# Preparing the first batch by halves: when tokens are turned, when query and key halves start, and when the value weights are split

## The reference

```python
mod = (silu(c) @ wmod).reshape(2, 6, 1, 256)
sa, ca, ga, sb, cb, gb = ...                       # shifts, scales and gates of a batch
h = layernorm(x) * (1 + ca) + sa
q, k, v = h @ query_proj, h @ key_proj, h @ value_proj   # 16 heads, 16 wide (q, k), 64 wide (v)
x = x + ga * (softmax(q @ k.T / 4, axis=queries) @ v) @ output_proj
h = layernorm(x) * (1 + cb) + sb
x = x + gb * fp4_ffn(h)                            # gate, up and down, quantised to FP4 in blocks of 16
```

## Time and profile before

| what | value |
|---|---|
| median of 3 runs | 1666.05 us (1665.92 to 1666.1) |
| the profiled execution's own time | 1665.84 us |
| its span in the trace | 1664.5 us |
| PE, DVE, ACT, POOL busy over the span | 98%, 94%, 83%, 46% |
| first scores of batch 0 start at | 70.6 us |

### The profile page before, as it was taken

The page is one execution under the profiler, slowest core; times in us unless marked ns, Lnnn a source line. Parts: engine busy times, 40 slices in busy tenths (PEclk is TensorE's granted clock), DMA queues, the critical chain, the costliest instruction groups (busy, mean ns, idle before and its releaser), DMA issues.

```text
span 1664.5 us, 38879 instructions
## 1 busy us (share of the span) xinstructions
PE 1634.2 (98%) x15435; PEld 796.8 (48%) x15435; DVE 1566.7 (94%) x1719; ACT 1377.4 (83%) x2557; POOL 773.6 (46%) x1624
## 2 busy tenths in 40 slices
PE   8999999999999999999999999999999999999999
PEld 7742223322322332673222332222233279999998
DVE  7899999999999999769999999999999969998887
ACT  6599999999999999659999999999999943343334
POOL 3034444444444445303545454566644456654552
DMA  7102111112111112511111112111111454444420
GB/s 243 58 11 73 51 48 46 45 52 67 51 51 53 46 46 77 153 55 40 48 50 45 46 45 71 51 51 52 48 46 45 133 159 127 153 127 133 148 91 23
DMA packets 83109, 123.15 MB, mean 74 GB/s; under 512 B 4712, under 2 KB 69104, under 8 KB 82928
## 3 DMA queue, kind: packets, MB, share of 16 engines
q1 hardware_dynamic: 82512, 120.15, 22.8%
q10 hardware_dynamic: 416, 0.53, 0.1%
HBM read 74.52 MB, written 46.15 MB: 72 GB/s over the span
## 4 chain that ended last, share of the span: by engine, by line
PE 90%; ACT 4%; DVE 2%; POOL 2%; issue 2%; DMA 0%; ACTq 0%; POOLq 0%
PE acc L641 53%; PE slot L612 14%; PE acc L473 12%; PE slot L473 9%; ACT e_sb L929 1%; PE slot L761 1%; ACT ost L951 1%; ACT ost L953 1%; DMA v_sb<-in_wmod 0%; PE slot L494 0%; PE acc L674 0%; POOL e_sb L1611 0%; DVE e_sb L1179 0%; PE acc L713 0%; ACT e_sb L858 0%
## 5 line engine op out<-in xcount | busy, mean ns | idle before, releaser
L1228 DVE TENSOR_REDUCE nm<-slot 128x1 f32<-128x1024 f32 x1024 | 1162.2, 1210 | 18.0 <-PE slot L612 18.0
L929 ACT ACTIVATE e_sb<-slot,nm 128x1024 f32<-128x1024 f32 x1024 | 1132.7, 1124 | 12.5 <-DVE nm L1228 12.5
L641 PE MATMUL acc<-e_sb,vp 64*64 64x512 f32 x8192 | 1065.1, 595 | 20.8 <-ACT ost L953 19.2
L612 PEld LDWEIGHTS slot<-stq,stk 64*64 64x64 f16 x4096 | 115.8, 103 | 674.2 <-ACT e_sb L929 639.6
L612 PE MATMUL slot<-stq,stk 64*64 64x512 f16 x4096 | 404.8, 387 | 0.0
L641 PEld LDWEIGHTS acc<-e_sb,vp 64*64 64x64 f32 x8192 | 281.4, 132 | 147.3 <-issue 58.0
L1545 POOL TENSOR_TENSOR dlt<-nm 128x4 f32<-128x4 f32 x128 | 25.6, 200 | 548.0 <-DVE nm L1228 548.0
L929 ACT ACTIVATION_READ_ACCUMULATOR e_sb<-slot,nm 128x1 f32 x1024 | 215.2, 210 | 0.0
L1536 POOL TENSOR_TENSOR vp<-v_sb,fac 128x512 f32<-128x512 f32 x128 | 133.4, 1042 | 10.2 <-POOL fac L1526 0.3
L1522 POOL TENSOR_TENSOR rtot<-tot,mone 128x4 f32<-128x4 f32 x128 | 132.7, 1036 | 10.0
L1084 POOL TENSOR_TENSOR ost<-ost,ost_hi 128x256 fp32r<-128x256 f32 x128 | 93.4, 730 | 10.3
(11 more groups left out here) (225 smaller groups left out, 1941.5 us busy)
## 6 DMA issues: line engine op xcount, KB each, us to landing
o_r<-o_heads SPq DMA_DIRECT2D x32, 1024.0 KB, 7.2
stk<-qk_parts SPq DMA_DIRECT2D x128, 128.0 KB
o_heads<-ost_hi SPq DMA_DIRECT2D x64, 256.0 KB, 3.4
o_heads<-ost SPq DMA_DIRECT2D x64, 256.0 KB, 4.0
v_sb<-in_x SPq DMA_DIRECT2D x16, 512.0 KB, 6.4
qk_parts<-e_sb SPq DMA_DIRECT2D x32, 256.0 KB, 2.4
stq<-qk_parts SPq DMA_DIRECT2D x128, 64.0 KB
out<-e_sb SPq DMA_DIRECT2D x32, 128.0 KB, 1.8
```

What stands on the lines that cost most here:

```text
L612: mm = pe.matmul(slot[s][side * VD:(side + 1) * VD, c * 512:(c + 1) * 512], stk[c * 64:c * 64 + 64, h % 2, i * P + side * VD:i * P + (side ...
L641: mm = pe.matmul(acc[half * VD:(half + 1) * VD, c * 512:(c + 1) * 512], vp[rows, g % 3, gi, half, :], e_v[rows, j % ERING, n0:n0 + 512], s ...
L929: act.activation(e_v[:, j % ERING, half * 1024:(half + 1) * 1024], slot[u % 3][:, :], ACT.Exp, bias=nm[:, g % 4, i, half:half + 1], accum_ ...
L1228: dve.tensor_reduce(nm[:, g % 4, i, half:half + 1], slot[u % 3][:, :], AX.X, ALU.max, negate=True).then_inc(maxed.sem)
```

## The change

For the first batch, and in part for both:

- `turn_tokens` signals `tok_turned` behind each half k (four transposes), `take_tokens` makes `hT` and `hT_hi` of one half before the other and signals `tok_out` for each half, `low_tokens` subtracts one half (128x512) at a time and signals for each. All waits on these semaphores count double.
- For b = 0 PE runs `queries_keys_by_half(g, pair, turned)`: for the pair of query results, then for the pair of key results, half k = 0 of both (six matmuls), then half k = 1 of both. Between the halves of the key pair it turns the tokens of group g + 1. So group g + 1 is turned inside group g, for all g.
- The 6 idle transposes ahead of the first turn and the 14 behind `bounds` are gone.
- On ACT, b = 0: half 0 of group 1 is taken ahead of group 0's parts, half 1 behind its second part; groups 2 and 3 are taken behind the second part of groups 1 and 2. The cast of the value weights comes behind group 1's parts, not group 0's.
- On DVE, b = 0: `stats` is cut into `block_stats` and `merge_stats`, `level` into `ratio` and `level`; the work of groups 1, 2 and 3 stands at other places between the parts (see the diff). `normalise(0, 3)` is behind the parts of group 1. `mod_rows_dve` comes ahead of step 10, not 13.
- For b = 1 the orders stay; only the halves' signals and the two smaller subtractions are new.

```diff
@@ turn_tokens, take_tokens, low_tokens
-            mm.then_inc(tok_turned.sem)
+                mm.then_inc(tok_turned.sem)
-            act.wait_ge(*tok_turned.past(b * NG + g))
-            for dst in (hT[g], hT_hi[g]):
-                for k in range(2):
+            for k in halves:
+                act.wait_ge(*tok_turned.past(2 * (b * NG + g) + k))
+                for dst in (hT[g], hT_hi[g]):
                     ins = act.activation(dst[:, k, :], z[:, k * 512:(k + 1) * 512], ACT.Identity,
                                          bias=sa[:, k, b:b + 1], scale=a1[:, k, b:b + 1])
-            ins.then_inc(tok_out.sem)
+                ins.then_inc(tok_out.sem)
-        def low_tokens(b, g):
-            dve.wait_ge(*tok_out.past(b * NG + g))
-            low(dve, hT_lo[g][:, :, :], hT[g], hT_hi[g][:, :, :]).then_inc(tok_low.sem)
+        def low_tokens(b, g, k):
+            dve.wait_ge(*tok_out.past(2 * (b * NG + g) + k))
+            low(dve, hT_lo[g][:, k, :], hT[g][:, k, :], hT_hi[g][:, k, :]).then_inc(tok_low.sem)
@@ PE
+        def queries_keys_by_half(g, pair, turned):
+            w_lo, w_hi = (wk_lo, wk_hi) if pair else (wq_lo, wq_hi)
+            for k in range(2):
+                if k and turned:
+                    turn_tokens(0, turned)
+                pe.wait_ge(*tok_low.past(2 * g + k))
+                for rows in range(2):
+                    n = 4 * g + 2 * pair + rows
+                    o = quarter_of(0, "qk", n) if k else take_quarter(0, "qk", n)
+                    cols = slice(rows * P, (rows + 1) * P)
+                    pe.matmul(o, w_hi[:, k, cols], hT_hi[g][:, k, :], start=(k == 0), stop=False)
+                    pe.matmul(o, w_lo[:, k, cols], hT_hi[g][:, k, :], start=False, stop=False)
+                    mm = pe.matmul(o, w_hi[:, k, cols], hT_lo[g][:, k, :], start=False, stop=(k == 1))
+                    if k:
+                        mm.then_inc(qk_mm.sem)
-                idle_turns(acc, 14)
-            for g in range(NG):
-                pe.wait_ge(*tok_low.past(b * NG + g))
-                if b == 0 and g == 0:
-                    pe.wait_ge(*wqk_low.past(0))
+                pe.wait_ge(*wqk_low.past(0))
+                for g in range(NG):
+                    queries_keys_by_half(g, 0, None)
+                    queries_keys_by_half(g, 1, g + 1 if g + 1 < NG else None)
-            idle_turns(acc, 6)
@@ prepare_act
             for g in range(NG):
+                if b == 0 and g == 0:
+                    take_tokens(0, 1, (0,))
                 for r in range(4):
                     part_act(b, g, r)
-                    if b == 0 and g == 0 and r == 1:
-                        take_tokens(0, 1)
-                if g + 2 < NG:
+                    if b == 0 and g + 1 < NG and r == 1:
+                        take_tokens(0, g + 1, (0, 1) if g else (1,))
+                if b and g + 2 < NG:
                     take_tokens(b, g + 2)
-                if b == 0 and g == 0:
+                if b == 0 and g == 1:
                     act.wait_ge(*got_wv.past(0))
                     high(wv_hi[:, :, :], wv_s[:, :, :]).then_inc(wv_high.sem)
@@ prepare_dve, b = 0
-                stats(0, 1)
-                low_tokens(0, 0)
+                low_tokens(0, 0, 0)
+                block_stats(0, 1)
+                low_tokens(0, 0, 1)
+                merge_stats(0, 1)
+                ratio()
                 normalise(0, 1)
                 level()
-                stats(0, 2)
+                block_stats(0, 2)
+                low_tokens(0, 1, 0)
             ...
                     if b == 0 and g == 0 and r == 1:
-                        normalise(0, 2)
-                        low_tokens(0, 1)
-                        stats(0, 3)
-                    if b == 0 and g == 0 and r == 3:
+                        merge_stats(0, 2)
+                        low_tokens(0, 1, 1)
+                    if b == 0 and g == 0 and r == 3:
+                        normalise(0, 2)
+                    if b == 0 and g == 1 and r == 1:
+                        low_tokens(0, 2, 0)
+                        block_stats(0, 3)
+                        low_tokens(0, 2, 1)
+                        merge_stats(0, 3)
+                    if b == 0 and g == 1 and r == 3:
                         normalise(0, 3)
+                    if b == 0 and g == 2 and r == 1:
+                        low_tokens(0, 3, 0)
+                        low_tokens(0, 3, 1)
             ...
-                if b == 0 and s == 13:
+                if b == 0 and s == 10:
                     mod_rows_dve()
```

## The result

The changed kernel takes 1669.34 us (median of 15, 1669.05 to 1673.44, all but one below 1669.9; that one has a mean granted clock of 0.997, the others 1.000) against 1666.1 us for the kernel before, measured with it (15 runs, 1665.92 to 1666.22). The ratio is 1.0021, 95% interval [1.0015, 1.0028]: 3.2 us slower. The forecast was 1668.1. The profiled execution took 1669.34 us with a span of 1668.0, 3.5 more than the 1664.5 of before.

The account below looks back on a forecast made before the run. PE bounds the kernel, with slack only before the first scores; 2.4 us later values less 0.3 regained gave +2.1 on 1665.84, so 1667.9, or 1668.1 with the median's 0.2; range 1664.2 to 1670.2.

Parts of the forecast that it names:

- The start: Before group 0: without the 6 idle transposes and with halves, first group matmul at 12.35, not 14.89, 2.5 us earlier.
- The lost cover: Turns between key halves: 2.9 us chain against 2.26 of PE work, so at least 0.63 us waited in three groups.
- The forecast's bound on what better order could win here: PE's waits between the first group matmul at 14.89 and the values at 41.85: 1.5 us.
- The collision: Group 3's normalisation on DVE meets POOL's value-weight subtractions on SBUF, released by cast and root together: 1.7 us later.
- Scores: First scores of batch 1's preparation window start at 72.7, against 70.6 before.
- The wait at 58.40: Stall of 0.15 us while values are made; gone because mod_rows_dve stands earlier, values taking 0.3 us less.
- VectorE's weight steps: DVE's end ahead of the scores moves 3.1 us to 68.9; PE wants the weights at 70.3, hidden by 1.4.
- Part 4: From the values on: 0.3 us less, DVE's weights stay hidden, stores and stack loads move by 3 us.
- the rival of full alternation: POOL and DVE alternate in group 3's normalisation and subtractions: values at 45.7, +3.5 us, 1669.6, up to 1671; chance 0.14.
- the 0.2%: Whole kernel's time: 3.3 us, about what a measurement can tell from no change; slower by more 0.17, same 0.75.
- Batch 1: Second batch's preparation: DVE's split subtractions cost 0.1 more each, but PE has no idle time there, so 0.
- the rival's small chance: PE's clock falls in a gap left by the idle transposes: 0.23 us more per group matmul, 1.5 more, 1669.6; chance 0.02.

Follow-up runs that it names:

- the new order: Changed kernel plus GpSimd waiting for group 3's normalisation, earlier row stores, turns ahead of key pairs; VectorE's and ScalarE's orders changed: 1664.03 us, 0.9988 of before.
- With cover and the changed kernel's order on VectorE: Changed kernel plus GpSimd waiting for group 3's normalisation, row stores ahead of second head's stacks, next group's turn ahead of the key pair: 1666.66 us, 1.0005 of before.
- the run without it: Changed kernel, but GpSimd starts its value-weight subtractions only after group 3's normalisation: 1668.02 us, 1.0012 of before.

## Why the prediction was right, and where it fell short

- *The start.* First matmul forecast at 12.35, measured 12.82. The 2.5 us were 2.1: VectorE waited for x until 5.17, so the first normalisation ended at 9.73, not 9.38. That isn't the change's doing: in the fourteen profiles of these kernels VectorE starts on x between 4.83 and 5.24 us, and the profile that the forecast was read from has the earliest. The order of the waits behind it was as forecast.
- *The lost cover.* Waits of 1.3, 0.6 and 0.9 ahead of groups 1, 2, 3 were forecast; 1.25, 0.46 and 0.73 of idle time were measured, plus 0.16 each for the modelled ends. Turn 2 needed no wait, as forecast. The forecast's bound on what better order could win here, 1.5 us, was too small: of the 26.96 us from the first group matmul to the values, 21.8 for matmuls and 2.4 for turns leave 2.7, and the new order takes 25.15 us (13.97 to 39.12). The runs also change the reading: the lack of cover isn't the cause by itself. With cover and the changed kernel's order on VectorE the time stayed at 1666.66; with cover and a new order it fell to 1664.03, on the same chip.
- *The collision.* Forecast: VectorE's normalisation of group 3 takes 1.7 us more. Measured: 1.58 more, and 1.3 us of the time by the run without it. The mechanism was right, the reason for its hour was not: I let cast and root share it, and expected a microsecond's delay of the cast to free it. The root alone decides, since GpSimd runs in order.
- *Scores.* Forecast at 72.7, measured at 72.72. That it fits to 0.02 us is partly luck: the values start at 44.48, 0.2 later than forecast, and 0.5 us was won back behind that, not 0.3. The wait at 58.40 is gone, as forecast; VectorE's weight steps ended at 69.16, 1.1 us ahead of their use at 70.23.
- *The step that failed* is in Part 4: "Stores and stack loads move by 3 us, as the scores do." They moved by 5.4, because the last part's store took 4.25 us to land and a wait for all parts stands behind it; and I followed them no further than to the scores. Behind the stacks stand four small stores that a copy needs some 14 us after the first scores. That they were in time before, by an estimated 1.6 us, I had not looked up. It is the term of the sum that was missing: +1.2 us, 1668.1 instead of 1669.3. The range held it, but the time came to lie next to the 1669.6 of the rival of full alternation, whose sign, values at 45.7, didn't come (44.48). The result lies at the edge of the 0.2%; 0.17 for slower than that was too little for a sum that had left a queue out.
- *Batch 1*: forecast 0. The shift is 3.46 us at 99.5 us and 3.5 at the end, so nothing is left for batch 1.
- *The clock*: in fourteen of fifteen executions of the changed kernel it held (mean granted clock 1.000), as the rival's small chance had it; the fifteenth, 1673.44 us with 0.997, looks like that rival come true, at 4.1 us instead of 1.5, but has no trace. Its price of 0.2 us a matmul was right, and the idle transposes do earn their place in the kernel before, which I gave little. The Trainium skill (TensorE: Matmul & The Clock Gate, Part 4: PE-mode transpose) has it that transposes don't count as busy for the gate. These runs disagree: on one chip the kernel before kept 1.000 in all of 32 executions, and without its 20 idle transposes in one of eleven. The opening transposes agree with the prediction's reading of them: the first 7 take 1.75 us and the other 19 of the 26 take 2.70. The granted clock reads 1.00 in that stretch throughout, so the level there is read from durations alone.

## What to carry to other kernels

An early start of the bound engine is worth nothing if it is paid for by putting off what the next rounds wait for: draw up each engine's list with its durations, and look for what the next round waits for, before splitting work finer. Follow a delayed producer through every queue behind it to the last wait that it can reach, stores of unrelated small data too, and look up how early they were. Beside a stream on GpSimd put VectorE's instructions that read PSUM (two parts took 1.40 us inside the stream, at 35.56, as outside it), and keep GpSimd's pieces small. Before crediting a loss to the clock, look for a second wait that the delay uncovers.

## What the runs showed of the hardware that I had not expected

- VectorE and GpSimd keep each other out by whole instructions when both work on SBUF data: four instructions of 0.4 us take 1.37 us alone, 2.96 beside pieces of 128x256, 5.12 beside pieces of 128x512. That they collide was forecast; that the size of the piece sets the price is what the runs add.
- TensorE's clock fell to the lower level behind idle stretches of 2.40 and 3.82 us, and once behind one of 0.80; it held behind 0.81 and 1.66 us in the changed kernel's profile, behind 1.66 in the new order's, and behind the 1.36 of before. What came ahead of the gap matters too, so the length of a gap alone doesn't tell; which rule decides stays open.
- Four stores of 2 KB took 9.8 us from the last issue to landing behind stack loads in the same queue, in four kernels (9.83 to 9.85).
- The wait for the last part's store to land took some 4.2 us in nine of the fourteen profiles, the kernel before without idle transposes among them, and 2.2 to 3.0 in the other five. What decides it, no run shows.
